# Attention on one core: the value sums of two macro steps issued together in every second step

## The reference

```python
q = jnp.einsum('bsd,hde->bshe', x, W_Q) + b_Q
k = jnp.einsum('bsd,hde->bshe', x, W_K) + b_K
v = jnp.einsum('bsd,hde->bshe', x, W_V) + b_V
scores = jnp.einsum('bqhe,bkhe->bhqk', q, k) / math.sqrt(D_HEAD)
scores = jnp.where(causal[None, None], scores, -jnp.inf)
pattern = jax.nn.softmax(scores, axis=-1)
z = jnp.einsum('bhqk,bkhe->bqhe', pattern, v)
attn_out = jnp.einsum('bqhe,hed->bqd', z, W_O) + b_O
```

## Time and profile before

| | us |
|---|---|
| median of 3 runs | 2604.02 |
| lowest and highest | 2603.34 and 2606.56 |
| the profiled execution's own time | 2611.85 |
| its span, first to last instruction | 2610.1 |
| attention stage, units 0 to 10 | 297.69 to 1656.27 of the span |
| attention stage, last unit | 1656.27 to 1759.36 |

### The profile page before, as it was taken

How to read it: one execution, slowest core, us unless ns; L and a number is a source line. 1 busy time by engine, 2 the same in 40 slices (tenths; PEclk the granted TensorE clock), 3 DMA queues, 4 the chain that set the end, 5 groups by cost and what they waited for, 6 DMA issues and landing times. The chain is left out here.

```text
span 2610.1 us, 42688 instructions
## 1 busy us (share of the span) xinstructions
PE 2367.1 (91%) x16192; PEld 1254.2 (48%) x16192; DVE 1879.4 (72%) x3802; ACT 1245.5 (48%) x1760; POOL 1245.2 (48%) x858
## 2 busy tenths in 40 slices
PE   3564899999999999999999999986999999999998
PEld 1233566666656565656666666543333333333332
DVE  7864665756565756656565657678888988988987
ACT  3322233333333333333333333346777777777776
POOL 6000166767575757676666667553413413323120
PEclk9787899999999999999999999996999999999999
DMA  1002000000001000000000001131010001000000
GB/s 51 12 12 66 1 8 1 10 7 4 9 1 34 1 10 1 10 1 10 1 10 1 10 1 20 19 57 52 9 27 19 9 19 21 15 19 18 10 7 7
DMA packets 42941, 39.35 MB, mean 15 GB/s; under 512 B 26865, under 2 KB 35186, under 8 KB 41842
## 3 DMA queue, kind: packets, MB, share of 16 engines
q1 hardware_dynamic: 40608, 31.18, 5.4%
q0 software_dynamic: 1536, 3.15, 0.5%
q10 hardware_dynamic: 594, 2.31, 0.2%
HBM read 26.13 MB, written 10.49 MB: 14 GB/s over the span
## 5 line engine op out<-in xcount | busy, mean ns | idle before, releaser
L690 POOL TENSOR_TENSOR acc<-acc,pT 128x1024 f32<-128x1024 f32 (+3 forms) x412 | 837.4, 2033 | 240.0 <-ACT pT L1131 203.7
L1131 ACT ACTIVATE pT<-banks 128x1024 f32<-128x1024 f32 x480 | 407.0, 897 | 768.4 <-PE banks L769 690.4
L1868 DVE TENSOR_TENSOR hw<-hid,banks 128x512 f32<-128x512 f32 x1024 | 663.3, 680 | 85.2 <-PE banks L1551 70.8
L930 DVE TENSOR_REDUCE part<-banks 128x2 f32<-128x1024 f32 (+3 forms) x432 | 438.2, 1044 | 283.8 <-PE banks L745 281.6
L1710 ACT ACTIVATE hid<-banks 128x1024 f32<-128x1024 f32 x512 | 496.7, 1022 | 185.3 <-PE banks L1541 168.4
L785 PE MATMUL banks<-pT,v 128*64 128x512 f32 (+3 forms) x1920 | 404.5, 542 | 2.4 <-DVE total L978 1.7
L1551 PE MATMUL banks<-wT,select 64*128 64x512 f16 x1024 | 342.5, 393 | 41.3 <-DVE hw L1868 21.8
L1541 PE MATMUL banks<-zst,w1c 50*128 50x512 f32 x1024 | 306.4, 542 | 11.8 <-ACT hid L1710 11.8
L1551 PEld LDWEIGHTS banks<-wT,select 64*128 64x128 f16 x1024 | 93.9, 94 | 399.2 <-DVE hw L1868 339.2
L1559 PE MATMUL banks<-hw,w 128*32 128x512 f32 x2048 | 278.8, 617 | 0.9 <-DVE hw L1868 0.9
L785 PEld LDWEIGHTS banks<-pT,v 128*64 128x64 f32 x1920 | 116.7, 136 | 191.8 <-issue 175.6
(11 more groups left out here) (243 smaller groups left out, 3241.9 us busy)
## 6 DMA issues: line engine op xcount, KB each, us to landing
zst<-z_scratch SPq DMA_DIRECT2D x48, 128.0 KB, 4.1
z_scratch<-zp SPq DMA_DIRECT2D x8, 512.0 KB, 2.8
out_h<-o SPq DMA_DIRECT2D x8, 384.0 KB, 2.6
xT_scratch<-xs_hi SPq DMA_DIRECT2D x4, 512.0 KB, 2.7
xt_hi<-xT_scratch SPq DMA_DIRECT2D x2, 1024.0 KB, 5.6
w<-in_L_ffn_W ACTq DMA_DIRECT2D x1, 2048.0 KB, 8.7
xt_hi<-in_L_ffn_W SPq DMA_DIRECT2D x12, 128.0 KB, 4.7
v<-in_L_ffn_W SPq DMA_DIRECT2D x12, 128.0 KB, 4.4
```

The source lines that it names most:

```text
L690: pool.tensor_tensor(acc[:, G % 2, :, off:CH], acc[:, G % 2, :, off:CH], pT[:, slot, :, 0:w], ALU.add).then_inc(summed, 1)
L930: last = dve.tensor_reduce(to[:, :, c:c + 1], both[:, :, 0:whole], AX.X, ALU.max)
L1131: act.activation(pT[:, J % PSLOTS, :, 0:CH - off], both[:, :, 0:CH - off], ACT.Exp, scale=E ** -0.5)\
L1868: dve.tensor_tensor(hw[:, n % 2, q, :], hid[:, n % 2, q, :], ring_bank(("w", g, n, q)), ALU.mult).then_inc(mixed, 1)
```

## The change

In every even macro step but the very first, TensorE now makes the value sums of four blocks, those of the two steps before; in odd steps it makes none. After the last unit's last step the four blocks that are left follow. The scores, the side items, the denominators, the ring, the slots and all other engines' lists stay as they are.

```diff
@@ -849,16 +849,15 @@
                     score_columns(it, 2 * t + 1)
                     for item in PLAN[it][t]:
                         side(item)
-                    if t:
-                        weigh(it, 2 * t - 2)
-                        weigh(it, 2 * t - 1)
-                    elif it:
-                        weigh(it - 1, NK - 2)
-                        weigh(it - 1, NK - 1)
+                    if t % 2 == 0 and (it or t):
+
+                        unit, first = (it, 2 * t - 4) if t else (it - 1, NK - 4)
+                        for j in range(first, first + 4):
+                            weigh(unit, j)
                     if behind(it, t, 1):
                         add_up(*behind(it, t, 1))
-            weigh(LAST, NK - 2)
-            weigh(LAST, NK - 1)
+            for j in range(NK - 4, NK):
+                weigh(LAST, j)
             add_up(LAST, NQC - 1)
             output(LAST, NQC - 1)
```

## The result

The changed kernel takes 2684.16 us (median of 4 runs, 2682.73 to 2685.60) against 2605.29 us (4 runs) for the kernel before: a ratio of 1.030, with a 95% interval of 1.0284 to 1.0316. It is slower, as forecast, but by about 79 us where 41 were forecast, and it lies outside the range (2598 to 2670). The profiled executions, 2683.63 and 2611.85 us, have spans of 2681.9 and 2610.1 us. What follows explains these 71.8 us; the kernel before ran some 7 us above its median in its profiled execution, and no row here shows where those lie.

The account below looks back on a forecast made before the run. TensorE was taken to set the time. Eleven units at +3.80 us (+41.8) and the last unit at -1 gave +40.8 us, so 2644.8 us; range 2598 to 2670 for 8 in 10, the forecast case's own 2621 to 2665.

Parts of the forecast that it names:

- the saved passages: Odd macro steps lose two switches between score and value matmul forms: 0.35 us each step, 120 steps, 42 us.
- The rival that nothing is saved: First score pair pays its 0.22 us after side items too, so no saving: 2687 us; chance 0.03.
- the one that the passages alone count: VectorE finishes within two score blocks, TensorE never stops for it: 42 us less, 2562 us; chance 0.13.
- the ring as the deciding limit: After odd steps TensorE needs score banks VectorE has not read: 7.3 us new waits per unit against 3.5 saved.
- nine of the ten borders: Odd-to-even step passages except 19 to 0: losses 1.49 (9-10), 0.86 (5-6), 0.45 (1-2); six others sum to -0.18 us.
- the borders that the forecast had as gains: Steps 3 to 4 gain 0.33 us, 7 to 8 gain 0.09, 17 to 18 gain 0.21, per unit.
- The argument on step 8: Longer step 8 does not relieve VectorE: its cast still ends with GpSimd's additions, leaving 1.49 us loss at 9 to 10.
- the rival of half the waits: Step 8's cast slips between two additions, step 10 waits 0.5 us, not 1.7: about 2620, all halved 2604; chance 0.10.
- GpSimd's additions were not late for the masks: Judges the rival that GpSimd overruns at quarter ends: 2 us more a unit, 2667 to 2690 us; chance 0.04.
- loss 1.50 - 0.32 = 1.18: Steps 19 to 0: 1.50 us of values moved, turned maxima at most 0.35 earlier, 0.32 taken; loss per unit.
- I take -1 us: Last unit: saved passages and wait ahead of step 7 some 2.6 us, less 1.5; bounds -5 to +1.5.
- the beginning of a rival: Range's upper end takes in the start of GpSimd's late-masks case, 2667 to 2690 us, chance 0.04.

Follow-up runs that it names:

- Light reads: Changed kernel with VectorE's unmasked reduces over half their columns: 2576.33 us, against 2588.20 us for the kernel before with the same halved reduces.

## Why the prediction was right, and where it was wrong

**Right: the saved passages.** 0.35 us each; the grouped pair that meets no wait got 0.31 us shorter in the mean (17+18 above). The rival that nothing is saved falls, and with it the one that the passages alone count: the gain is there and is outweighed.

**Right: the ring as the deciding limit, and nine of the ten borders.** Reading VectorE's ends off the timeline, putting TensorE 0.05 us behind them and comparing with the old start gave 2.62 us per unit against 2.77 measured. Light reads turn the sign, and the borders that the forecast had as gains are gains when done alone. The argument on step 8, that the cast asks earlier but inside the same run of additions, held, and the rival of half the waits falls with it. GpSimd's additions were not late for the masks: no wait of the values (L785) stands in the eleven units.

**Wrong: "loss 1.50 - 0.32 = 1.18" for steps 19 to 0.** It measured 3.68. The step took VectorE's product as ending at its old time, and set 0.03 us aside for the neighbouring instructions on GpSimd. But with the values gone from step 19, step 0's scores, and with them the exponential that releases GpSimd's copy, come earlier against VectorE's maxima, so the copy meets the product: 0.8 us. (The copy begins 2.8 us behind step 0's first scores in either kernel; the product began 1.3 us behind them and now begins 2.9 behind.) The prediction had read this hold on the cast of step 8 and did not ask the same of the second small instruction. Then the wait of 1.9 us was followed by the lower clock in 10 of 11 cases, 1.67 us each, for which the prediction had no term. No row of before showed either in units 1 to 11, but unit 0, whose step 0 has no values to make, showed both in the trace of before:

```profile
300.50 1.03 POOL L687 COPY acc<-pT 128x1024 f32<-128x1024 f32 x1
300.62 0.95 DVE L949 TENSOR_TENSOR cpad<-negmax,cpad 128x8 fp32r<-128x8 f32 x1
...
301.71 0.63 PE L753 MATMUL banks<-ident,cpad 128*128 128x128 f32 x4 [1.92 <-DVE cpad L949]
...
302.00:308.00 6.00, 6.00 (x30) 4.53 (x29) 0.44 (x1) 1.58 (x3) 4.81 (x6) 0.52 0.01 3
```

The same copy holds the same product, TensorE waits the same 1.9 us, and behind it, with no run of values, the granted clock is 0.52. Over eleven units the two make 10 x 2.5 + 0.8 = 26 us of the 31 by which the span's difference exceeds the forecast.

**Wrong: "I take -1 us" for the last unit.** It measured +3.1, beyond the bound of +1.5. Its normalising wait in step 3 did go, and it was 2.8 us ahead at step 12's start; but the chain through VectorE to step 12's second scores kept all but 0.3 of that, and the four blocks of values ahead of a quarter's denominators put these off, +1.2 net. Then VectorE's last preparation for the next stage began behind an addition of GpSimd (before, it began 0.44 us ahead of one):

```profile
1808.73 3.20 POOL L690 TENSOR_TENSOR acc<-acc,pT 128x1024 f32<-128x1024 f32 x1
...
1809.65 4.43 DVE L1036 SCALAR_TENSOR_TENSOR w1c<-w1c,is_low,v 128x2048 fp32r<-128x2048 f32 x1
...
1811.89 2.46 POOL L674 TENSOR_SCALAR_AFFINE_SELECT pT<-pT 128x256 f32<-128x256 f32 x1
...
1815.00 0.58 PE L765 MATMUL banks<-zst,ones 64*128 64x256 f32 x2 [4.24 <-DVE h_all L985]
```

It took 4.43 us, before 2.49, and step 19's first scores wait 4.24 us where they waited 2.19. With the old order the last unit is 3.2 us shorter, as the run on it showed; which of these rows holds how much of it was not separated.

**The range.** Its upper end, 2670, stood for waits 25% longer than read (2665) and the beginning of a rival. The clock costs some 17 us for the ten drops; without them the result would have been near 2667, within it.

## What to carry to other kernels

Taking out work from an engine that sets the time pays only where nobody used that work as a pause: list the ring's readers and the time of each release before and after, border by border, and make the change only at the borders where the reader is ahead; here three of ten gave 0.26%, all ten cost 3%. When an instruction moves against another engine's list, ask of every small instruction on the path to the next release what it will now stand beside. And price a new wait on TensorE not at its length alone: the work right behind it may run at the lower clock.

## What was not expected of the hardware

A product over 128x8 elements took 0.95 us in place of 0.17 beside a copy of GpSimd, and 0.17 again when the copy was held back. A cast of the same size took up to 2.15 us and ended with GpSimd's additions; no run took these away, so there the cause is read from the ends alone. Waits of this kind stand in the profile as busy time of VectorE.

The lower clock came after waits of 1.9 and 1.5 us, in a stage where the granted clock was 1.00 before; in the kernel with three borders grouped, which has neither wait in units 1 to 11, no step of theirs had it. It followed 10 of 11 such waits in the changed kernel and 2 of 11 identical ones with step 9 as before; it fell in step 10 of units 1 to 4, behind a wait of 1.5 us, and in step 0 of units 6 and later in the run with the last unit's order undone, in which a unit took 129.6 to 130.1 us. Where the wait at step 0 was 1.2 or 0.3 us, no step 0 had it. So the wait matters, but does not decide alone. The Trainium skill, "TensorE: Matmul & The Clock Gate", HAM oscillation, tells of a kernel whose waits between bursts of matmuls, there for transfers, bring the lower clock again and again; that much agrees. What decides between one unit and the next stays open.
